# Causal mask of the row scores added by VectorE inside PSUM, both heads' maxima by one operation; first FFN GEMM's copies on ScalarE; two rotation buffers

## What is computed

```python
q = query @ wq + query @ Aq @ Bq * LORA_SCALE      # k, v alike (k without the low-rank part)
q, k = apply_rope(q, sin, cos), apply_rope(k, sin, cos)
scores = jnp.einsum('bhqd,bhkd->bhqk', q, k) / jnp.sqrt(dh)
scores = jnp.where(causal, -1e9, scores)
out = jnp.einsum('bhqk,bhkd->bhqd', softmax(scores), v) @ wo
x = layernorm(x + out)
h = butterfly(x @ W_exp + b_exp, up_weights)
h = butterfly(gelu(h + up_bias), down_weights)
x = layernorm(x + h @ W_con + b_con + down_bias)
```

## Time and profile before

| what | us |
|---|---|
| median of 3 runs | 1289.97 (1289.91 to 1305.36) |
| the profiled execution, its own time | 1295.52 |
| its span, first to last instruction | 1293.8 |
| TensorE matmuls busy | 1162.7 (90%) |
| VectorE busy | 828.9 (64%) |
| ScalarE busy | 677.0 (52%) |
| GpSimd busy | 470.7 (36%) |
| mean granted TensorE clock (share of 2.4 GHz) | 0.946 |

### The profile page before, as it was taken

The page is one execution under the profiler, slowest core; times in us unless marked ns, Lnnn a source line. Parts: engine busy times, 40 slices in busy tenths (PEclk is TensorE's granted clock), DMA queues, the critical chain, the costliest instruction groups (busy, mean ns, idle before and its releaser), DMA issues.

```text
span 1293.8 us, 25961 instructions
## 1 busy us (share of the span) xinstructions
PE 1162.7 (90%) x7822; PEld 794.1 (61%) x7822; DVE 828.9 (64%) x1954; ACT 677.0 (52%) x1067; POOL 470.7 (36%) x520
## 2 busy tenths in 40 slices
PE   4477779989999999999999999999999999989876
PEld 3344446656666666756666666766666666656465
DVE  5387867666766767575766766676766666665232
ACT  1146546555474737465564747465654747463601
POOL 2231334434443434444344334443343443332310
PEclk9567779999999999999999999999999999999889
DMA  5736363444646463644546363745545464631110
GB/s 195 171 108 165 89 161 94 160 113 151 152 125 167 119 176 100 182 120 146 123 142 172 117 164 92 201 112 164 127 152 128 125 176 126 168 93 51 52 42 33
DMA packets 94981, 169.86 MB, mean 131 GB/s; under 512 B 14872, under 2 KB 36120, under 8 KB 94944
## 3 DMA queue, kind: packets, MB, share of 16 engines
q1 hardware_dynamic: 93888, 166.53, 47.6%
q10 hardware_dynamic: 832, 1.83, 0.4%
q0 software_dynamic: 224, 1.04, 0.2%
HBM read 92.28 MB, written 77.07 MB: 131 GB/s over the span
## 4 chain that ended last, share of the span: by engine, by line
PE 64%; DVE 14%; DMA 10%; issue 8%; SPq 2%; ACT 1%; POOL 1%; DVEq 1%; POOLq 0%; ACTq 0%
PE ps_m L516 21%; PE ps_m L654 15%; PE ps_m L624 9%; PE ps_t L596 7%; DMA x_res<-in_x 6%; PE ps_s L584 5%; PE ps_s L558 5%; DVE m_raw L843 3%; DMA qk_scr<-rot 3%; DVE m_raw L838 3%; DVE stats L901 1%; DVE rope_in L862 1%; SPq L453 1%; DVE x_res L916 1%; PE ps_m L616 1%
## 5 line engine op out<-in xcount | busy, mean ns | idle before, releaser
L727 ACT ACTIVATE pT<-ps_t 128x512 f32<-128x512 f32 x640 | 345.9, 600 | 295.4 <-PE ps_t L596 294.9
L843 DVE TENSOR_REDUCE m_raw<-ps_s 128x1 f32<-128x512 f32 (+2 forms) x768 | 344.9, 503 | 181.8 <-PE ps_s L584 180.5
L987 POOL TENSOR_SCALAR_AFFINE_SELECT pT<-pT 128x512 f32<-128x512 f32 (+1 forms) x320 | 174.4, 549 | 414.5 <-ACT pT L727 413.7
L654 PE MATMUL ps_m<-w,gact 128*128 128x256 f32 x1024 | 234.8, 381 | 1.8 <-ACT gact L795 1.1
L654 PEld LDWEIGHTS ps_m<-w,gact 128*128 128x128 f32 x1024 | 188.9, 190 | 26.0 <-ACT gact L795 1.5
L558 PE MATMUL ps_s<-k_st,q_st 48*128 48x512 f32 (+3 forms) x1024 | 139.3, 330 | 42.6 <-DVE m_raw L843 22.3
L596 PE MATMUL ps_t<-q_st,k_st 50*128 50x512 f32 (+3 forms) x1024 | 170.4, 391 | 0.0
L624 PE MATMUL ps_m<-pT,v_aug 128*32 128x512 f32 (+3 forms) x2048 | 164.7, 466 | 5.9 <-DVE rope_in L862 2.7
L596 PEld LDWEIGHTS ps_t<-q_st,k_st 50*128 50x128 f32 x1024 | 82.7, 188 | 102.1 <-issue 96.5
L558 PEld LDWEIGHTS ps_s<-k_st,q_st 48*128 48x128 f32 x1024 | 97.3, 195 | 54.8 <-DVE m_raw L843 31.5
L624 PEld LDWEIGHTS ps_m<-pT,v_aug 128*32 128x32 f32 x2048 | 60.8, 115 | 91.0 <-issue 85.1
(11 more groups left out here) (112 smaller groups left out, 1578.4 us busy)
## 6 DMA issues: line engine op xcount, KB each, us to landing
qk_scr<-rot_hi SPq DMA_DIRECT2D x64, 512.0 KB, 3.3
q_st<-qk_scr SPq DMA_DIRECT2D x128, 192.0 KB, 4.6
k_st<-qk_scr SPq DMA_DIRECT2D x128, 192.0 KB, 5.1
qk_scr<-rot SPq DMA_DIRECT2D x32, 512.0 KB, 4.2
o_scr<-o_raw SPq DMA_DIRECT2D x64, 256.0 KB, 2.1
r_b<-in_xT SPq DMA_DIRECT2D x17, 512.0 KB, 7.9
o_c<-o_scr SPq DMA_DIRECT2D x32, 256.0 KB
r_b<-r_scr SPq DMA_DIRECT2D x32, 256.0 KB
```

The costliest lines, as they stand in the source:

```text
L654: mm = pe.matmul(pm[:, 0:D], gact[:, k, n * P:(n + 1) * P], w2[:, k, :], start=(k == 0), stop=(k == NHT - 1))
L727: act.activation(pT[:, g % 2, slot, half * T:(half + 1) * T], ps_t[:, ST_BANK[2 * n + r], :], ACT.Exp, scale=SCALE).then_inc(exp_done, 1)
L843: ins = dve.tensor_reduce(m_raw[:, r, u // 2, qt:qt + 1], ps_s[:, r, off:off + (qt + 1) * P], AX.X, ALU.max, negate=True)
L987: pool.affine_select(out=v, in_=v, compare_op=ALU.is_ge, fill=0.0, base=0, pattern=pattern, channel_multiplier=-1).then_inc(mask_done, 1)
```

## The change

- The mask matmuls (L584) are gone with their bf16 operands and the transfer of the mask. GpSimd builds a 128x128 triangle `tri` once. For each unit VectorE waits until both heads' scores are there, adds `tri` in place in PSUM (256 elements per partition for both heads in units 0 and 2, 512 in the others) and then reduces both heads by one operation (1024 elements; in units 1 and 3 two, of 768 and 256).
- All eight copies of a W1 tile are made by ScalarE; before, the odd ones were VectorE's.
- "MT" moves from `front` to `back` of the same steps (2, 7, 12, 17).
- `rot` and `rot_hi` have two buffers, "LOW" is cut in two parts per rotation (four entries, in steps 3, 4, 6, 7), "HIGH" 1 and "QKH" 1 move from step 6 to 5, and "QKL" 1 from step 7 to step 8, ahead of "FILL" 0 and behind "MROW" 2 and "RAW" 0.
- "XLO" is cut in two parts (steps 15, 16), "BIAS" in two parts (steps 17, 18; before one, in step 15).

```diff
-    front = {0: [("QK", i + 1, 1)], 1: [("W1", i - 2, 7)], 2: [("QK", i + 1, 2), ("MT", i, 1)],
+    front = {0: [("QK", i + 1, 1)], 1: [("W1", i - 2, 7)], 2: [("QK", i + 1, 2)],
...
-             7: [("W2B", i - 2, 2), ("MT", i, 2)], 8: [("PV", i, 0)], 9: [("W2", i - 2, 3)],
-             10: [("WO", i - 1, 0)], 11: [("WO", i - 1, 1)], 12: [("V", i + 1, 0), ("MT", i, 3)],
+             7: [("W2B", i - 2, 2)], 8: [("PV", i, 0)], 9: [("W2", i - 2, 3)],
+             10: [("WO", i - 1, 0)], 11: [("WO", i - 1, 1)], 12: [("V", i + 1, 0)],
...
-    back = {0: [("W1", i - 2, 6)], 4: [("W2", i - 2, 0)], 5: [("W2", i - 2, 1)], 6: [("W2", i - 2, 2)],
+    back = {0: [("W1", i - 2, 6)], 2: [("MT", i, 1)], 7: [("MT", i, 2)], 12: [("MT", i, 3)], 4: [("W2", i - 2, 0)], 5: [("W2", i - 2, 1)], 6: [("W2", i - 2, 2)],
...
-            17: [("W1", i - 1, 5)]}
+            17: [("W1", i - 1, 5), ("MT", i + 1, 0)]}
...
         if t == 2:
             put("HIGH", i + 1, 0)
-            put("LOW", i + 1, 0)
         if t == 3:
             put("QKH", i + 1, 0)
+            put("LOW", i + 1, 0)
...
         if t == 4:
+            put("LOW", i + 1, 1)
             put("ROPE", i + 1, 1)
-        if t == 6:
+        if t == 5:
             put("HIGH", i + 1, 1)
             put("QKH", i + 1, 1)
-            put("LOW", i + 1, 1)
+        if t == 6:
+            put("LOW", i + 1, 2)
         if t == 7:
             put("XRES", i - 1, 0)
+            put("LOW", i + 1, 3)
+        if t == 8:
             put("QKL", i + 1, 1)
-        if t == 8:
             put("FILL", i + 1, 0)
...
+                mm = s_mm(r, 2 * P * x, x, 1, x == 0)
+                if x == GP - 1:
+                    mm.then_inc(s_done, 1)
...
-                        pe.matmul(o, identb[:, :], m, start=False, stop=True,
-                                  skip_group_check=True).then_inc(s_done, 1)
...
+                    dve.wait_ge(s_done, 2 * (NU * b + n + 1))
...
+                    dve.tensor_tensor(v, v, m, ALU.add).then_inc(s_masked, 1)
+                    dve.wait_ge(s_masked, NU * b + n + 1)
+                    if u == GH:
+                        ins = dve.tensor_reduce(m_raw[:, :, :, 1],
+                                                ps_s[:, :, :].rearrange("p r (x c) -> p r x c", x=GP),
+                                                AX.X, ALU.max, negate=True)
+                    else:
+                        for off, qt in ((0, 3),) if u % 2 == 0 else ((0, 2), (3 * P, 0)):
+                            ins = dve.tensor_reduce(m_raw[:, :, u // 2, qt:qt + 1],
+                                                    ps_s[:, :, off:off + (qt + 1) * P],
                                                     AX.X, ALU.max, negate=True)
...
-                elif kind == "W1" and n % 2 == 0:
+                elif kind == "W1":
```

More of the change, by code:

```diff
@@ L171, in steps @@
             put("XHI", i + 2, 0, B + 1)
-            put("BIAS", i - 1)
+            put("XLO", i + 2, 0, B + 1)
             put("FILL", i + 1, 2)
         if t == 16:
-            put("XLO", i + 2, 0, B + 1)
+            put("XLO", i + 2, 1, B + 1)
+        if t == 17:
+            put("BIAS", i - 1, 0)
         if t == 18:
+            put("BIAS", i - 1, 1)
             put("OUT", i - 2)
@@ L484, in one @@
                     if n == 0:
[L486 removed]
+                        hold(sp, xl_done, 2 * (min(b + 3, B + 1) if isinstance(b, int) else b + 3))
                     sp.dma_start(r_b[:, n, :],
@@ L522, in evacuated @@
             def evacuated(kind, b, n):
-                if kind == "W1":
-                    wait(pe, evac_w1[n % 2], NHT // 2 * b + n // 2 + 1)
-                else:
-                    wait(pe, evac[kind], PER[kind] * b + n + 1)
+                wait(pe, evac[kind], PER[kind] * b + n + 1)
             def one(step):
@@ L553, in one @@
                         pe.wait_ge(fill[g], FILLN * (b + 1))
-                    wait(pe, max_done, 2 * (NU * b + n))
+                    wait(pe, max_done, NU * b + n)
                     def s_mm(r, off, x, qt, start):
@@ L559, in s_mm @@
                                          q_st[rows, pr, qt * P:(qt + 1) * P],
-                                         k_st[rows, pr, 0:(qt + 1) * P], start=start, stop=False,
+                                         k_st[rows, pr, 0:(qt + 1) * P], start=start, stop=True,
                                          skip_group_check=True)
@@ L573, in one @@
                         for r in range(2):
-                            s_mm(r, 3 * P, u // 2, 0, False)
-                    for r in range(2):
-                        if u == GH:
-                            o = ps_s[:, r, :].rearrange("p (x c) -> p x c", x=GP)[:, :, P:2 * P]
-                            m = maskb[:, :].rearrange("p (x c) -> p x c", x=GP)
-                        elif u % 2 == 0:
-                            o, m = ps_s[:, r, 3 * P:4 * P], maskb[:, 0:P]
-                        else:
-                            o, m = ps_s[:, r, 2 * P:4 * P], maskb[:, :]
-                        pe.matmul(o, identb[:, :], m, start=False, stop=True,
-                                  skip_group_check=True).then_inc(s_done, 1)
+                            s_mm(r, 3 * P, u // 2, 0, False).then_inc(s_done, 1)
                 elif kind == "ST":
@@ L834, in one @@
                         wait(dve, msplit, 2 * (NG * b + g))
-                    for r in range(2):
-                        dve.wait_ge(s_done, 2 * (NU * b + n) + r + 1)
-                        if u == GH:
-                            ins = dve.tensor_reduce(m_raw[:, r, :, 1],
-                                                    ps_s[:, r, :].rearrange("p (x c) -> p x c", x=GP),
-                                                    AX.X, ALU.max, negate=True)
-                        else:
-                            for off, qt in ((0, 3),) if u % 2 == 0 else ((0, 2), (3 * P, 0)):
-                                ins = dve.tensor_reduce(m_raw[:, r, u // 2, qt:qt + 1],
-                                                        ps_s[:, r, off:off + (qt + 1) * P],
-                                                        AX.X, ALU.max, negate=True)
-                        ins.then_inc(max_done, 1)
+                    dve.wait_ge(s_done, 2 * (NU * b + n + 1))
@@ new lines, in one @@
+                    m = tri[:, :].unsqueeze(1).broadcast_to([P, 2, P]) if u < GH and u % 2 == 0 else \
+                        tri[:, :].unsqueeze(1).unsqueeze(1).broadcast_to([P, 2, 2, P])
+                    if u == GH:
+                        v = ps_s[:, :, :].rearrange("p r (x c) -> p r x c", x=GP)[:, :, :, P:2 * P]
+                    elif u % 2 == 0:
+                        v = ps_s[:, :, 3 * P:4 * P]
+                    else:
+                        v = ps_s[:, :, 2 * P:4 * P].rearrange("p r (x c) -> p r x c", x=2)
@@ L965, in _ @@
             pool.memset(mhalf[:, :], -0.5)
+            pool.memset(tri[:, :], 0.0).then_inc(tri_c, 1)
+            pool.wait_ge(tri_c, 1)
+            pool.affine_select(out=tri[:, :], in_=tri[:, :], compare_op=ALU.is_ge, fill=-1e30, base=0,
+                               pattern=[[-1, P]], channel_multiplier=1).then_inc(tri_c, 1)
             pool.memset(v_aug[:, :, :, :], 1.0).then_inc(pool_c, 1)
@@ L1010, in one @@
                     pool.wait_ge(done["XT"], KD * (b + 1))
-                    pool.wait_ge(c_ready, 3)
-                    pool.tensor_tensor(x_res[:, :, :], x_res[:, :, :],
-                                       bias_out[:, :].unsqueeze(1).broadcast_to([P, NT, D]), ALU.add)\
+                    pool.wait_ge(c_ready, 1)
+                    rows = x_res[:, 2 * n:2 * n + 2, :]
+                    pool.tensor_tensor(rows, rows, bias_out[:, :].unsqueeze(1).broadcast_to([P, 2, D]), ALU.add)\
                         .then_inc(x1b_done, 1)
@@ L1100 @@
     theta = np.repeat(theta.T.astype(np.float64), H, axis=0)
-    tri = np.where(np.arange(P)[None, :] > np.arange(P)[:, None], np.float32(-1e30), np.float32(0))
     arrays = {
@@ L1118 @@
         "ident": np.eye(P, dtype=np.float32),
-        "mask": np.concatenate([tri, tri], axis=1),
     }
```

79 lines of the change are left out of this document (36 added, 43 removed).

## The result

| | before | after |
|---|---|---|
| median of the runs | 1289.94 us (4 runs) | 1384.24 us (4 runs) |
| ratio after / before | | 1.0705, 95% interval 1.0613 to 1.0797 |
| span of the profiled execution | 1293.8 us | 1383.1 us |
| mean granted clock | 0.946 | 0.908 |

The account below looks back on a forecast made before the run. TensorE was taken to lead most of the turn, except around `x_res` in steps 9 to 14. 36.0 + 14.7 + 25.1 = 75.8 us against 71.3, +4.5 over 14 turns, +63: 1353 us, range 1275 to 1392.

Parts of the forecast that it names:

- A: From "PV" of step 3 to VectorE's "WO" 1, when `x_res` has landed: 33.25 us a turn becomes 36.0.
- Rival 1: SyncE's queue doesn't delay `x_res`: turn 71.3 us, time 1290, or 1310 with half of the delay; chance 0.25.
- masks gone: Mask matmuls taken out, priced at 0.32 or 0.22 us a pair on the chain: TensorE 5.6 us a turn lighter.
- Rival 2: Faster, VectorE's add nearly free or hidden: 1244; the masks alone could give down to 1200; chance 0.15.
- Part C: From "S" of step 15 to the next "PV" of step 3: 25.06 us a turn becomes 25.15.
- Part B: From VectorE's "WO" 1 to "S" of step 15: 12.97 us becomes 14.7, by dearer units 19, 0 and 1.
- VectorE's share: What VectorE's dearer adds and merged maxima cost outside the queue: 1.8 of the 4.5 us a turn.
- Rival 3, the clock: The clock falls to half at each new stall, also at the short waits of Part C: 1405; chance 0.1.
- Costed at nothing: Two rotation buffers, "LOW", "XLO" and "BIAS" in parts: hidden or off the path, no cost.

Follow-up runs that it names:

- a_qkl7: The changed kernel with "QKL" 1 back in step 7, ahead of "MROW" 2 in SyncE's queue: 1355.63 us, ratio 1.0510.
- a_pemask: The changed kernel with mask matmuls and separate maxima back; order, buffers and ScalarE's W1 copies stay: 1319.62 us, ratio 1.0235.
- a_both: The changed kernel with "QKL" 1 back in step 7 and all four "MT" back in `front`: 1334.57 us, ratio 1.0372.
- b_nomask: The kernel before without its mask matmuls and nothing in their place, row scores unmasked: 1278.46 us, ratio 0.9897.
- b_x1b_nomask: b_x1b without the mask matmuls and nothing in their place, row scores unmasked: 1242.85 us, ratio 0.9650.
- b_dvemask: The kernel before with only the mask added by VectorE in PSUM and merged maxima: 1350.73 us, ratio 1.0500.
- b_dvemask_low: b_dvemask with GpSimd's "LOW" cut in two parts, one rotation buffer: 1354.06 us, ratio 1.0511.
- b_x1b: The kernel before with "BIAS" writing to a tile of its own, so both "XRES" go out in step 1: 1261.73 us, ratio 0.9787.
- a_noadd: The changed kernel without the add of the mask, row scores unmasked, merged maxima kept: 1309.39 us, ratio 1.0125.
- a_warm: The changed kernel with 15 additional matmuls in step 12, meant to keep TensorE at work during the stall: 1385.77 us, ratio 1.0757.

## Why the prediction was right, and where its terms were not

**The direction and the mechanism of A were right; how well its number fits is luck.** "QKL" 1 behind "MROW" 2 is what SyncE waits on, and `x_res` goes out 31.16 us after "PV", inside the 30.1 to 31.2 that were worked out. But two errors lie in that agreement. "QKL" lands in 2.8 us (median 2.9 over all turns), less than the shortest that the trace before had shown (3.3). Of "QKL" 1 alone the median is 2.9 after, 3.5 in a_qkl7, where it has its old place in the order, and 4.6 before; so its place makes 0.6 of it, and the rest goes with the other changes, which no run parts. Without more, `x_res` would go out at 29.5, as in the turn from 863.10. The other 1.7 us are "PV" 3 at half clock. Set right, the queue holds `x_res` 2.45 us a turn over "W2E" 3 (31.16 against 28.71; a_pemask 1.9, before 0.3). In a_pemask that is 1.8 of the 2.8 us a turn behind its 33; in the kernel after, "QKL" back in its place gives 25 us and with "MT" 43, both with what the clock gives back beside it (a_qkl7, a_both). "W2E" 3 itself was put 1.6 us earlier and is 0.3 earlier at full clock, 1.3 later where "PV" 3 is slow. Rival 1, that the queue wouldn't hold `x_res`, didn't come about.

**The term "masks gone" was mis-sized by a factor of three.** Step "Prices, masks gone": 0.32 and 0.22 us a pair, 5.6 us a turn. b_nomask gives 0.65 for the eight pairs of C, against 2.3; b_x1b_nomask 1.75 a turn for all twenty, against 5.6. Of the prediction's terms this one is furthest off: it set 5.6 us a turn against VectorE's dearer units where there were 1.75. The error was to take a price from the chain of waits, which books the whole stretch between two tiles on what runs there. Only a kernel without the masks made the right number visible, as the distance from "S" to the next "ST". Rival 2's floor of 1200 for the masks alone falls with it.

**Part C** was put at 25.15 and is 26.37. This is the largest miss of the three parts, 1.2 us. Its three waits are there as worked out (0.67 for the W1 copy, foretold 0.7; 1.05 before "PV" 3, foretold 1.2; small ones in steps 19 and 0). With 0.65 instead of 2.3 for the masks the same sum is 26.8.

**Part B** was put at 14.7; it is 14.59 to 14.67 in four turns of a_qkl7, where "PV" 1 takes 3.5 to 4.0 us and VectorE still covers that, and 15.1 to 15.4 in three turns after, where it takes 4.1 to 4.4. The VectorE chain was right to the tenth (14.67 also in the turns of a_both and b_dvemask whose "PV" 1 is at full clock), and the clock came on top.

**VectorE's share.** The prediction had 2.75 of its 4.5 us a turn from the queue and 1.8 from VectorE. The parts alone say 33 us for the order and 64 for VectorE. What was missing on VectorE's side: the masks' small worth and the clock. The split that runs into GpSimd's "LOW" was missing too, but b_dvemask_low shows no time for it.

**Rival 3, the clock**, got 0.1 and was in part what happened: 1.7 us at "PV" 3 in nine of eleven turns and 0.9 on average in B (15.64 over 14.7), together 2.3 us a turn. The kernel before loses 0.35 a turn in B the same way (13.32 over 12.97), so 2.0 of the 6.9 us a turn are the clock, about 28 of the 94 us. The prediction weighed it on part B only, where it is nearly covered, and asked of C only that its short waits might bring it down. "PV" 3 does fall, but the wait ahead of it doesn't decide it (see "The clock"), and what does stays open.

**Costed at nothing, as far as the runs show rightly:** buffers, "LOW", "XLO" and "BIAS" in parts. One of them has a price off the path: VectorE's scaling of y rose from 0.405 to 0.630 us; it now stands beside "BIAS" on GpSimd (1.79 us for two from 686.74, "BIAS" 1.31 from 686.75). That the four cost the path nothing is inferred, since a_pemask's loss is accounted for without them; none was run by itself.

## What to carry to other kernels

Price an instruction that is to be taken out by the distance between its neighbours with and without it, not by its busy time or its share of the chain: here 116 us of busy matmuls were worth 12 and 18, each known to about 10. When work moves from a nearly full engine to a half full one, look for the places where the two are chained through one buffer; a unit that may only start when the last one has been drained turns each tenth on the second engine into a tenth of the whole. And an entry moved behind a waiting one in an in-order queue costs not itself but everything behind it (here one entry, 25 us).

## What was not expected of the hardware

- A VectorE copy of 16 columns took 2.22 us beside a GpSimd operation of 2.34 us, and 1.15 beside one of 1.27, ending with it both times; 0.17 us when alone.
- 640 bf16 mask matmuls with 116 us of busy time between fp32 tiles cost 12 us in one kernel and 18 us in another (b_nomask against before, b_x1b_nomask against b_x1b, each to about 10 us); without them the following tile took 0.10 us longer in the step shown.
- A fall to 1.2 GHz costs 1.7 us for one "PV" of 32 matmuls (4.05 instead of 2.36 us), and it occurs in some turns and not in others of the same loop, so that turns of one kernel differ by up to 5 us (a_qkl7: 74.4 to 79.5, the longest with a second fall in B). The length of the wait just ahead of it doesn't tell: 0 of 11 turns at 0.9 us (a_noadd), 9 and 4 of 11 at 1.05 us (after, a_warm), 3 of 11 at 0.39 us (b_dvemask).
- Fifteen additional matmuls in the stall didn't keep the clock up: it was granted 0.50 while they ran, and they took 5.25 us (a_warm).
- In-place adds in PSUM cost VectorE the same as adds from PSUM to SBUF of that size (0.697 and 0.692 us for 512, 0.426 and 0.424 for 256).
